# Two graph-attention layers that aggregate by row halves of 64, with a dot product, a normalisation and a diagonal in another order

## The reference

```python
x = _layernorm(x + _L0_gnn_ref(x, adj, ...))      # layer 0
x = _layernorm(x + _L1_gnn_ref(x, adj, ...))      # layer 1: 4 heads, output attention, feed-forward
x = _layernorm(x + _L2_gnn_ref(x, adj, W, a_src, a_dst))
x = _layernorm(x + _L3_gnn_ref(x, adj, W, a_src, a_dst))

def _L2_gnn_ref(x, adj, W, a_src, a_dst):         # _L3_gnn_ref is the same
    Wh = jnp.einsum('bnd,de->bne', x, W)
    e_src = jnp.einsum('bnd,d->bn', Wh, a_src)
    e_dst = jnp.einsum('bnd,d->bn', Wh, a_dst)
    logits = e_src[:, :, None] + e_dst[:, None, :]
    logits = jnp.where(logits >= 0, logits, NEG_SLOPE * logits)
    logits = jnp.where((adj == 0)[None, :, :], -jnp.inf, logits)
    attn = jnp.nan_to_num(jax.nn.softmax(logits, axis=-1), nan=0.0)
    return jnp.einsum('bnm,bmd->bnd', attn, Wh)
```

## Time and profile before

| what | value |
|---|---|
| median of 3 runs | 3140.3 us (3139.85 to 3141.08) |
| the profiled execution | 3139.89 us |
| its span, first to last instruction | 3138.2 us |
| mean granted TensorE clock | 0.993 of full speed |
| busy over the span: TensorE / weight loads / VectorE / ScalarE / POOL | 98% / 86% / 73% / 57% / 66% |
| DMA over the span | 78 GB/s |
| chain that ended last | TensorE 76%, issue 5%, POOL 3% |

### The profile page before, as it was taken

How to read it: one execution, slowest core, us unless ns; L and a number is a source line. 1 busy time by engine, 2 the same in 40 slices (tenths; PEclk the granted TensorE clock), 3 DMA queues, 4 the chain that set the end, 5 groups by cost and what they waited for, 6 DMA issues and landing times.

```text
span 3138.2 us, 64986 instructions
## 1 busy us (share of the span) xinstructions
PE 3074.8 (98%) x19593; PEld 2691.9 (86%) x19593; DVE 2297.8 (73%) x4825; ACT 1776.1 (57%) x4325; POOL 2061.9 (66%) x2773
## 2 busy tenths in 40 slices
PE   8999989999999999999999999999899999999997
PEld 6888878889988888898889889888688888888885
DVE  6777656777777776777777777765788888888886
ACT  3333335555555555555555555543577777777775
POOL 5666635666666666666666656641688888888886
PEclk9999999999999999999999999999899999999999
DMA  6555411111111111111111111114332333223220
GB/s 198 178 190 177 151 46 40 41 50 50 47 53 40 53 40 55 45 47 53 47 47 40 60 40 47 53 41 155 91 97 82 100 94 97 86 91 100 90 74 28
DMA packets 181766, 244.46 MB, mean 78 GB/s; under 512 B 15808, under 2 KB 81344, under 8 KB 181696
## 3 DMA queue, kind: packets, MB, share of 16 engines
q1 hardware_dynamic: 169920, 218.46, 21.5%
q10 hardware_dynamic: 9216, 16.78, 1.4%
q0 software_dynamic: 2560, 8.39, 0.8%
HBM read 159.68 MB, written 83.89 MB: 78 GB/s over the span
## 4 chain that ended last, share of the span: by engine, by line
PE 76%; issue 5%; POOL 3%; ACT 1%; DVE 1%; DMA 0%; SPq 0%; POOLq 0%; ACTq 0%; DVEq 0%
PE wop L2020 23%; PE hp L2006 20%; PE wop L47 9%; PE hp L2171 5%; PE hp L47 5%; PE agg L1989 4%; PE shared L2028 2%; PE agg L2131 2%; PE shared L2131 2%; POOL w_first L1223 1%; PE shared L248 1%; PE hp L2158 1%; POOL g_terms L1291 1%; PE smallp L200 1%; POOL cols L389 0%
## 5 line engine op out<-in xcount | busy, mean ns | idle before, releaser
L1223 POOL TENSOR_TENSOR w_first<-xd,v_row 128x512 f32<-128x512 f32 x480 | 682.5, 1435 | 346.1 <-DMA xd<-x_scratch 315.3
L2006 PE MATMUL hp<-yT_hi,big_hi 128*128 128x256 f32 x2048 | 595.1, 291 | 0.0
L2006 PE MATMUL hp<-yT_hi,big_lo 128*128 128x256 f32 x2048 | 580.1, 283 | 0.0
L2006 PE MATMUL hp<-yT_lo,big_hi 128*128 128x256 f32 x2048 | 579.8, 283 | 0.0
L2020 PE MATMUL wop<-big_hi,hT_hi 128*128 128x512 f32 x1024 | 424.8, 415 | 0.4 <-ACT v_row L1404 0.4
L2020 PE MATMUL wop<-big_hi,hT_lo 128*128 128x512 f32 x1024 | 402.1, 393 | 0.0
L2020 PE MATMUL wop<-big_lo,hT_hi 128*128 128x512 f32 x1024 | 400.5, 391 | 0.0
L2006 PEld LDWEIGHTS hp<-yT_hi,big_hi 128*128 128x128 f32 x2048 | 392.8, 192 | 7.5 <-DVE yT_lo L1698 0.7
L2006 PEld LDWEIGHTS hp<-yT_lo,big_hi 128*128 128x128 f32 x2048 | 392.7, 192 | 3.0 <-issue 0.2
L2006 PEld LDWEIGHTS hp<-yT_hi,big_lo 128*128 128x128 f32 x2048 | 392.7, 192 | 0.0
L1291 POOL TENSOR_TENSOR g_terms<-x,g_v_row 128x512 f32<-128x512 f32 x256 | 368.1, 1458 | 35.3 <-ACT x L1557 33.5
(11 more groups left out here) (218 smaller groups left out, 8115.2 us busy)
## 6 DMA issues: line engine op xcount, KB each, us to landing
x0f<-in_x_turned SPq DMA_DIRECT2D x64, 256.0 KB, 2.7
xt<-in_x SPq DMA_DIRECT2D x64, 256.0 KB, 2.9
x_scratch<-w_first ACTq DMA_DIRECT2D x64, 256.0 KB, 2.2
xa<-x_scratch SPq DMA_DIRECT2D x64, 256.0 KB, 2.7
att_hi_scratch<-att_hi SPq DMA_DIRECT2D x64, 256.0 KB, 2.0
att_lo_scratch<-who SPq DMA_DIRECT2D x64, 256.0 KB, 2.0
att_scratch<-attT SPq DMA_DIRECT2D x64, 256.0 KB, 2.0
att_hi<-att_hi_scratch SPq DMA_DIRECT2D x64, 256.0 KB, 3.7
```

The costliest lines, as they stand in the source:

```text
L1223: nc.gpsimd.tensor_tensor(terms[:, k % TR, :], xd[:], v_row[:, k, :], ALU.mult).then_inc(terms_ready, 1)
L2006: ins = nc.tensor.matmul(hp[half][:, s * 2 * P:(s + 1) * 2 * P], a, b, start=c == 0 and i == 0, stop=c == KC - 1 and i == 2)
```

## The change

There are three parts.

1. Aggregations in row halves. `turned` becomes 128 rows by 64 columns: each graph's block lies at its own rows and there are no zero blocks, so `pool_zero` is gone. `aggregate3` issues for each 128 features two matmuls, of rows 0 to 63 and of rows 64 to 127, each with 64 moving columns, into the two banks of `agg`. Layers 2 and 3 share these banks, each with half of the columns; the small results of layer 2 move to `shared`. Because the banks are shared, each aggregation also waits until VectorE has read the other layer's last one. The splits (`agg_hi3`, `agg_lo`) read through a permuted view. The last two tiles of layer 1's output attention are aggregated in the same way (`last_sums`, `last_exp`), and their place in the first steps moves: ScalarE does `last_exp` and `split_att` ahead of `turned3(g2, 0)`, VectorE `out_elu` earlier, and TensorE waits for `att_ready` before the first `aggregate3(g2)`.
2. ScalarE writes layer 2's normalised tile (`normalise3`) ahead of both of layer 2's dots, where it stood between them.
3. POOL builds layer 2's diagonal (`diag3(g2)`) between the two products of layer 3, where it stood ahead of both.

```diff
-        self.turned = piece(6 * NODES, P)
+        self.turned = piece(6 * NODES, NODES)
...
     def act_turned(self, nc, act, t):
         act.wait_ge(self.turned_done, t + 1)
-        if isinstance(t, int) and t == 0:
-            act.wait_ge(self.zeroed, 1)
         for g in range(2):
             r = slice(g * NODES, (g + 1) * NODES)
-            nc.scalar.copy(self.turned[r, :, r], self.turned_psum[r, :, r]).then_inc(self.turned_ready, 1)
+            nc.scalar.copy(self.turned[r, :, :], self.turned_psum[r, :, r]).then_inc(self.turned_ready, 1)
...
-            agg_2, agg_3 = (bank.rearrange("p (c n) -> p c n", c=KC) for bank in (agg[:, 0, :], shared[:]))
-            small_2, small_3 = agg[:, 1, :], smallp[:]
+            agg_2, agg_3 = (agg[:, :, q * KC * NODES:(q + 1) * KC * NODES].rearrange("p g (c n) -> p g c n", c=KC)
+                            for q in range(2))
+            small_2, small_3 = shared[:], smallp[:]
...
                     if live(n, 1):
                         for k in range(2):
                             products3(g2, n - 1, k, x2[(r - 1) % R][:], x2_ready)
+                    if live(n, 3):
+                        products3(g3, n - 3, 0, x3[(r - 3) % R][:], g2.x_ready)
+                    if live(n, 1):
                         diag3(g2, n - 1)
                     if live(n, 3):
-                        for k in range(2):
-                            products3(g3, n - 3, k, x3[(r - 3) % R][:], g2.x_ready)
+                        products3(g3, n - 3, 1, x3[(r - 3) % R][:], g2.x_ready)
...
-            nc.scalar.copy(g.aggS[0][:], g.agg[:]).then_inc(g.agg_hi_ready, 1)
+            nc.scalar.copy(by_graph(g.aggS[0][:]), g.agg).then_inc(g.agg_hi_ready, 1)
...
                     if live(n, 1):
                         ge(act, g2.z_ready, n - 4)
                         normalise3(n_1, n - 1, z1[:], x2[(r - 1) % R][:], x2_ready)
+                    if isinstance(n, int) and n == 2:
+                        last_exp(T - 1)
+                        split_att(T - 1, PAIRS)
                     if live(n, 2):
                         turned3(g2, n - 2)
...
-                    if live(n, 1):
-                        dot3(g2, n - 1, 0)
                     if live(n, 3):
                         ge(act, g3.z_ready, n - 6)
                         normalise3(g2.norm, n - 3, g2.z[:], x3[(r - 3) % R][:], g2.x_ready)
                     if live(n, 1):
+                        dot3(g2, n - 1, 0)
                         dot3(g2, n - 1, 1)
-                    if isinstance(n, int) and n == 2:
-                        out_exp(T - 1)
-                        split_att(T - 1, PAIRS)
...
                 def aggregate3(g, t, x):
                     pe.wait_ge(g.att.turned_ready, 2 * t + 2)
-                    ge(pe, g.agg_lo_ready, t)
                     for c in range(KC):
-                        ins = nc.tensor.matmul(g.agg[:, c, :], x[:, c * P:(c + 1) * P], g.att.turned[:, 0, :],
-                                               start=True, stop=True)
+                        for b in range(2):
+                            own = slice(b * NODES, (b + 1) * NODES)
+                            ins = nc.tensor.matmul(g.agg[:, b, c, :], x[own, c * P:(c + 1) * P],
+                                                   g.att.turned[own, 0, :], start=True, stop=True)
                     ins.then_inc(g.agg_done, 1)
...
                     if live(n, 5):
+                        pe.wait_ge(g2.agg_lo_ready, capped(n - 2, T))
+                        ge(pe, g3.agg_lo_ready, n - 5)
                         aggregate3(g3, n - 5, x3[(r - 5) % R])
...
                     if live(n, 2):
+                        if isinstance(n, int) and n == 2:
+                            pe.wait_ge(att_ready, T)
+                        if live(n, 5):
+                            pe.wait_ge(g3.agg_lo_ready, n - 4)
+                        ge(pe, g2.agg_lo_ready, n - 2)
                         aggregate3(g2, n - 2, x2[(r - 2) % R])
```

More of the change, by code:

```diff
@@ L328, in __init__ @@
         self.turned_done, self.turned_ready = sem("turned_done"), sem("turned_ready")
-    def pool_zero(self, nc):
-        nc.gpsimd.memset(self.turned, 0.0).then_inc(self.zeroed, 1)
     def act_exp(self, nc, act, t):
@@ L1010, in gnn_stack_kernel @@
             g3 = Gat("g3", 3 * KC, agg_3, small_3, wop[1], g3_own, 256, g3_rows, g3_terms, g3_agg, g3_z)
-            g2.wide, g3.wide = wop, (wop[1], shared)
+            g2.wide, g3.wide = wop, (wop[1], smallp)
             weights = (w1, w2, W2, W3)
@@ L1033, in run, with by_graph, turned_att @@
                     step(p)
+            def by_graph(x):
+                return x.rearrange("p c (g n) -> p g c n", g=2)
+            def turned_att():
+                return attT[:].rearrange("p (c g n) -> p g c n", c=KC, g=2)
             def pair(p):
@@ L1388, in keep_wo, with last_exp @@
                     nc.scalar.copy(who[j][:], wop[j][:]).then_inc(who_ready, 1)
+                def last_exp(s):
+                    act.wait_ge(uo_done, s + 1)
+                    act.wait_ge(att_stored, 16 * s)
+                    nc.scalar.activation(turned_att(), agg_2, ACT.Exp).then_inc(exo_ready, 1)
                 def out_exp(s):
@@ L1667, in _ @@
                 ao_.act_exp(nc, act, 2 * m + 1)
-                out_exp(2 * m)
+                last_exp(2 * m)
                 keep_att(1)
@@ L1739, in out_elu @@
                     dve.wait_ge(nego_ready, s + 1)
+                    if isinstance(s, int) and s >= T - 2:
+                        nc.vector.tensor_tensor(turned_att(), agg_2, turned_att(), ALU.max).then_inc(att_ready, 1)
+                        return
                     nc.vector.tensor_tensor(attT[:], shared[:], attT[:], ALU.max).then_inc(att_ready, 1)
@@ L1843, in agg_lo @@
                     dve.wait_ge(g.agg_hi_ready, t + 1)
-                    nc.vector.tensor_tensor(g.aggS[1][:], g.agg[:], g.aggS[0][:].bitcast(F32), ALU.subtract
-                                            ).then_inc(g.agg_lo_ready, 1)
+                    nc.vector.tensor_tensor(by_graph(g.aggS[1][:]), g.agg, by_graph(g.aggS[0][:].bitcast(F32)),
+                                            ALU.subtract).then_inc(g.agg_lo_ready, 1)
                 def scores(g, t):
@@ L1926, in step3 @@
                         after_exp(g2, n - 2)
+                    if isinstance(n, int) and n == 2:
+                        out_elu(T - 1)
                     if live(n, 4):
@@ L1944, in step3 @@
                         g3.norm.dve_mean(nc, dve, n - 5, g3.x_ready)
-                    if isinstance(n, int) and n == 2:
-                        out_elu(T - 1)
                     if isinstance(n, int) and n == 3:
@@ L2125, in _, with last_sums @@
                 run(pe, step, first=0)
+                def last_sums(s, j):
+                    pe.wait_ge(ao_.turned_ready, 2 * s + 2)
+                    for c in range(KC):
+                        for b in range(2):
+                            own = slice(b * NODES, (b + 1) * NODES)
+                            ins = nc.tensor.matmul(agg_2[:, b, c, :], who[j][own, c * P:(c + 1) * P],
+                                                   ao_.turned[own, 0, own], start=True, stop=True)
+                    ins.then_inc(uo_done, 1)
                 def aggregate3(g, t, x):
                     pe.wait_ge(g.att.turned_ready, 2 * t + 2)
-                    ge(pe, g.agg_lo_ready, t)
                     for c in range(KC):
-                        ins = nc.tensor.matmul(g.agg[:, c, :], x[:, c * P:(c + 1) * P], g.att.turned[:, 0, :],
-                                               start=True, stop=True)
+                        for b in range(2):
+                            own = slice(b * NODES, (b + 1) * NODES)
+                            ins = nc.tensor.matmul(g.agg[:, b, c, :], x[own, c * P:(c + 1) * P],
+                                                   g.att.turned[own, 0, :], start=True, stop=True)
                     ins.then_inc(g.agg_done, 1)
@@ L2216, in step3 @@
                         pe.wait_ge(att_ready, T - 1)
-                        out_sums(T - 1, 1)
+                        last_sums(T - 1, 1)
                     if isinstance(n, int) and n == 3:
-                        pe.wait_ge(att_ready, T)
                         spread_rows(g3)
@@ L2246, in _ @@
                 first_half(2, 2)
-                out_sums(2 * m, 0)
+                pe.wait_ge(y_lo_ready, 8 * PAIRS)
+                last_sums(2 * m, 0)
                 pe.wait_ge(ao_.turned_ready, 2 * (2 * m + 1))
```

4 lines of the change are left out of this document (1 added, 3 removed).

## The result

The changed kernel takes 3197.3 us (median of 4 runs, 3195.66 to 3199.93) where the kernel before, run beside it, takes 3140.1. The ratio is 1.0183, 95% interval 1.0165 to 1.0200: slower by 57 us. The forecast was 3189 us in a range of 3168 to 3212. The profiled execution has a span of 3195.8 us at a granted clock of 0.992.

What follows compares the result with a forecast made beforehand. PE's own work bounds the steady steps: 56 x (0.63 + 0.16) = 44.2 us, with 2.7 for first and 2.0 for last steps 48.9, on the 3138.2 span, plus time around it: 3189 us, range 3168 to 3212.

Steps and rivals of the forecast that it cites:

- Row halves: Layers 2 and 3 aggregations on PE: seams cost 0.345 and 0.285 us, together 0.63 us a step more.
- The rival of a pace of 0.055 us: Aggregations: pairs run at their 64 columns' pace; 4% for faster, 5% for about 3140 to 3150 us.
- The credit of 0.055 for 64 moving columns: Half-row aggregations: only the last pair gets 0.055 us shorter, the pairs' pace stays at 0.11.
- Layer 2's diagonal: POOL builds it behind one layer 3 product, so PE waits 0.16 us a step before layer 2's spread.
- The anchors: Times after layer 3's transpose: POOL's product +1.79, layer 2's diagonal +3.04, its spread's weight load +3.38.
- the link from the diagonal to its load: Layer 2's diagonal start to its spread's weight load: 0.34 us, the floor taken from layer 3's link.
- The contended product: Rival: POOL's product runs into VectorE's work, 0.45 us more, wait 0.61 a step, 3214 us; 12%.
- Layer 3's diagonal: On POOL, at about +5.0 instead of +5.37 after layer 3's transpose; link safe, nothing to gain.
- The steady sum: Steady steps: 56 x (0.63 + 0.16) = 44.2 us more.
- First steps: Copies behind the moved exponential and split come later: +2.4 and 0.3 for seams, 2.7 us; bounds 0 and 5.
- the time from the last exponential to the split: ScalarE in step 2: 1.80 us, plus the split's 0.6, moves the copies about 2.4 us.
- Last steps: End of the kernel, where PE's idle time covers most of the 0.63: +2 us, bounds -1 and +5.

Runs made afterwards that it cites:

- ScalarE's order alone: Kernel before with only ScalarE's order changed, normalising layer 2's tile ahead of both of layer 2's dots: 3152.1 us, ratio 1.0030.
- the square parts with POOL's products held back: Changed kernel with 64x64 aggregation parts, layer 2's spread behind layer 3's aggregation, POOL's layer 2 products waiting for VectorE's low half of layer 1's tile: 3134.5 us.
- the same kernel without that wait: Changed kernel with aggregations in 64x64 parts and layer 2's spread behind layer 3's aggregation, without the wait on POOL's products: 3144.5 us, ratio 1.0006.
- POOL's order undone: Changed kernel with POOL building layer 2's diagonal ahead of both of layer 3's products again: 3189.2 us, ratio 1.0147.
- the halves alone: Changed kernel with ScalarE's and POOL's orders of the kernel before; the last exponential stays ahead of the copies: 3186.9 us, ratio 1.0139.
- the square parts and the old place of layer 2's spread: Row halves with the orders of before, each half-row matmul cut into two of 64 stationary columns, waits earlier: 3141.7 us, ratio 0.9998.
- the moved spread: Row halves with the orders of before, layer 2's full-row spread moved into the middle of layer 3's half-row aggregation: 3207.6 us, ratio 1.0209.

## Why the prediction was right, and where it was off

Against the span of before, 3138.2, the kernel after has 57.6 us more: 46.4 in 55 steady steps, 4.65 in the first steps, 3.4 in the last, and 3.1 ahead of the first transposes. The forecast had 48.9.

- *Row halves.* 0.345 for layer 2 and 0.285 for layer 3 were forecast; 0.345 and 0.290 were measured, as means of the distances over the steady steps. Both steps of the reasoning were tested apart: seams by adding two (+0.35), the stationary columns as the pace by halving them (0.84 to 0.48 us from first to last record). The rival of a pace of 0.055 us fell, by the argument that the earlier trace rows were taken for. The credit of 0.055 for 64 moving columns has the right size but another place: it isn't in the last pair but between the first two, 0.160 apart here and 0.213 in layer 1's group, while the way out is 0.540 in both.
- *Layer 2's diagonal.* The anchors were +1.79, +3.04, +3.38; they came at +1.76, +3.02, +3.43 in the mean. The wait is 0.21 us a step by the kernel without it, and 0.22 by the distances on PE (0.12 ahead of the spread, 0.10 inside it), not 0.16. The forecast put the 0.10 of the load ahead of the spread's first record, at +3.48 against +3.33 (a difference of 0.15, carried on as 0.16). Measured, the first record stands at its load, +3.44, and the 0.10 is behind it: the second comes at +3.60 in place of +3.38. The mis-sized piece is the link from the diagonal to its load, taken as 0.34 from layer 3's: it is 0.42 here. The contended product, the rival of +0.45, didn't come: this product takes 1.30.
- *Layer 3's diagonal* was put at about +5.0 and is at +4.50 in the mean, since the product ahead of it takes 1.27 and not the contended 1.74 of the earlier trace rows. "After the change this link is safe" held, but "there was nothing to gain there" was only half the reading. A link at its floor is also one that any delay hits: it made ScalarE's order alone cost 0.164 a step, which I expected to be free.
- *The steady sum.* 44.2 was forecast for 56 steps, 46.4 measured in 55.
- *First steps*, 2.7 forecast, 4.65 measured. The third step, in which the moved exponential lies, takes 22.69 us in place of 19.45, 3.24 more where the forecast had 2.4. The term that was mis-sized is the time from the last exponential to the split, taken as 1.80 from the earlier trace rows; it is 2.60 in the kernel after. VectorE's elu (its part of the activation) between the two has moved beside a POOL product. The kernel before, the kernel after, and the square parts with POOL's products held back (the last experiment), timeline:

```profile
2220.97 0.43 DVE L1737 TENSOR_SCALAR attT<-attT 128x512 f32<-128x512 f32 x1 [1.03 <-ACT attT L1393]
```

```profile
2219.40 0.59 ACT L1397 ACTIVATE attT<-agg 128x512 f32<-128x512 f32 x1
2219.70 2.66 POOL L1295 TENSOR_TENSOR g_terms<-x,g_v_row 128x512 f32<-128x512 f32 x2
2220.03 1.22 DVE L1745 TENSOR_SCALAR attT<-attT 128x512 f32<-128x512 f32 x1 [2.38 <-ACT attT L1397]
...
2222.00 0.62 ACT L1408 CAST att_hi<-attT 128x512 fp32r<-128x512 f32 x1 [2.01 <-DVE attT L1749]
...
2223.10 1.97 PE L2152 MATMUL agg<-g_own,x 64*128 64x64 f32 x16 [4.64 <-ACT g_own L347]
```

```profile
2218.03 0.43 DVE L1749 TENSOR_SCALAR attT<-attT 128x512 f32<-128x512 f32 x1 [2.38 <-ACT attT L1401]
```

  It is a collision with POOL again: 1.22 in place of 0.43, and 0.79 of the 0.80 are found. With POOL's products held back it is 0.43 once more, and the third step is 0.79 shorter than in the same kernel without that wait (21.08 against 21.87). The aggregation behind the copies waits 4.64 us for them. The kernel with POOL's order undone loses 3.6 us more in the first steps; part of that can be the clock, as said below.
- *Last steps*, 2 forecast, 3.4 measured, inside the bounds. The granted clock belongs to this, and the forecast didn't have it. The last steps of the kernel before, then of the kernel after, columns as in the earlier trace rows:

```profile
3059.10:3138.20 79.10, 60.02 (x295) 46.06 (x293) 50.01 (x139) 44.73 (x120) 48.71 (x100) 0.96 0.07 27
```

```profile
3113.30:3195.80 82.50, 65.79 (x383) 49.77 (x381) 49.70 (x136) 45.05 (x120) 47.17 (x100) 0.89 0.07 27
```

  The clock is at 1.2 GHz in place of 2.4 for 7.1 us of the first of these and for 17.6 us of the second. My estimate is that 10.5 us more at half the rate cost at most half of that, 5.2, which is more than the whole excess of 3.4. PE has waits in both stretches; how much of the 3.4 is the clock and how much is work that moved was not tested apart.
- *Ahead of the pipeline*, nothing forecast, 3.1 measured. Most of the code there is the same, and among the thirteen kernels profiled, this one and that before included, the first transposes lie between 2177.4 and 2183.5 us with no order to it. I take it for scatter of one profiled execution, which wasn't tested apart.

What stays open: why the halves alone lose 8 us in the first steps. They lose 3.4 more there than the kernel after, all in the fifth step (21.02 against 19.77) and the sixth (18.93 against 16.59). In the fifth PE waits 2.08 us for ScalarE's copy `att_n` in place of 1.04. In the sixth it is nearly always busy in both. The kernel after, then the halves alone, columns as in the earlier trace rows:

```profile
2260.00:2276.50 16.50, 16.46 (x103) 13.49 (x102) 12.33 (x30) 10.55 (x29) 10.48 (x18) 0.90 0.32 95
```

```profile
2259.20:2278.20 19.00, 19.00 (x104) 16.08 (x104) 11.05 (x30) 10.64 (x31) 10.51 (x17) 0.76 0.29 83
```

A clock of 0.76 over 19 us is some 9 us at 1.2 GHz, against some 3 of the kernel after; 6 us more at half the rate are up to 3, and 2.3 are to be explained. So the clock can be this loss, but no run was made to separate it. Nor do the rows tell which part of the last steps' loss belongs to which chain. With the square parts and the old place of layer 2's spread PE still waits some 0.11 us a step around layer 3's spread, which was not traced to its end.

## What to carry to other kernels

Price a split of the contraction rows by its two seams and by the stationary columns it loads, not by the columns it streams. Here eight pairs of 64x128 kept the pace of eight full records and cost 0.29 to 0.35 us more. Before swapping two producers on an engine that isn't the bound, list the slack of both links and of everything queued behind the one that now waits. And where a VectorE instruction with two operands in SBUF and a POOL product start within 0.1 us of each other, settle the order by a wait: here a start 0.06 us earlier or later decided over 1 us of VectorE's instruction, and the wait was worth 0.3% of the kernel. And look at the granted clock of each stretch, not only at its mean over the kernel: 0.992 over the whole hid 0.89 in the last steps.

## What the runs showed of the hardware that was not expected

- Four parts of 64x64 in fp32 run side by side: 32 records in 0.48 us, a set of four every 0.058; of 64x128 a pair every 0.11, with 64 moving columns as with 128.
- Going to the half rows and coming back costs 0.35 us together around layer 2's aggregation, 0.29 around layer 3's behind its spread, and 0.35 around the moved spread; leaving the square parts is 0.05 cheaper (0.148 from the last record to the next matmul, against 0.202).
- VectorE's two-input instruction of 128x512 takes 0.69 us alone and up to 1.82 beside a POOL product that started first or together with it (POOL's order undone); POOL's product takes 1.30, and 1.82 the other way round. A one-input TENSOR_SCALAR of 128x512 takes 0.43 alone and 1.22 beside a POOL product that started 0.33 us ahead of it.
